# The first pair's neighbour codes are made and read earlier in a two-layer graph kernel

## What is computed

```
# layer 0: for every node the 25 neighbours of lowest number
h = max(layernorm(x), 0)
scores = where(adj != 0, -arange(N), -inf)
vals, idx = top_k(scores, 25)
feats = where(vals > -inf, h[idx], -inf)         # (b, n, 25, c)
agg = feats.max(axis=2)
agg = where(degree <= 25, max(agg, 0), agg)
x = x + relu(concat([h, agg]) @ W0 + b0)
# layer 1: dense masked attention over the same graph
h = max(layernorm(x), 0)
hidden = h @ W1.T;  a1, a2 = hidden @ a.T
attn = leaky_relu(a1[:, :, None] + a2[:, None, :], 0.2)
attn = softmax(where(adj > 0, attn, attn - 1e12))
x = x + attn @ hidden + bias1
```

## Time and profile before

| what | us |
|---|---|
| median of 3 runs | 5479.37 |
| the runs | 5475.32 to 5479.76 |
| the profiled execution's own time | 5479.48 |
| its span, first to last instruction | 5477.6 |
| busy: GpSimd | 3051.7 |
| busy: VectorE | 2618.6 |
| busy: TensorE | 2595.7 |
| busy: ScalarE | 1562.9 |

### The profile page before, as it was taken

The page is one execution under the profiler, slowest core; times in us unless marked ns, Lnnn a source line. Parts: engine busy times, 40 slices in busy tenths (PEclk is TensorE's granted clock), DMA queues, the critical chain, the costliest instruction groups (busy, mean ns, idle before and its releaser), DMA issues.

```text
span 5477.6 us, 38224 instructions
## 1 busy us (share of the span) xinstructions
PE 2595.7 (47%) x8782; PEld 1579.9 (29%) x8782; DVE 2618.6 (48%) x6725; ACT 1562.9 (29%) x1745; POOL 3051.7 (56%) x3204
## 2 busy tenths in 40 slices
PE   2212244455444455454455544455534555545479
PEld 1101122233222233332233322233322333323246
DVE  5444455454545454544454445444445445445342
ACT  3011133232333232333232333232323232323135
POOL 5566656555556555555555555655555656556520
PEclk9755566677767677766677766676766677767689
DMA  7344446555556565555565555555554655555320
GB/s 255 104 152 155 154 145 182 157 178 152 163 161 184 158 184 146 162 165 180 158 180 148 161 163 175 166 154 166 161 167 156 184 149 183 152 157 166 120 93 28
DMA packets 477228, 866.03 MB, mean 158 GB/s; under 512 B 308298, under 2 KB 309204, under 8 KB 456660
## 3 DMA queue, kind: packets, MB, share of 16 engines
q0 software_dynamic: 153600, 419.64, 27.0%
q1 hardware_dynamic: 305140, 378.64, 21.5%
q10 hardware_dynamic: 18432, 67.12, 3.1%
HBM read 690.98 MB, written 119.54 MB: 148 GB/s over the span
## 4 chain that ended last, share of the span: by engine, by line
another core or an unknown queue 31%; PE 21%; issue 16%; DVE 14%; ACT 13%; SPq 2%; DMA 1%; POOL 1%; ACTq 1%; DVEq 0%; POOLq 0%
PE acc L1325 11%; ACT nm_t L560 7%; DVE highest L909 3%; DVE top L843 2%; PE bank L1258 2%; DVE key L849 2%; ACT wgt L596 2%; SPq L364 2%; PE bank L1238 2%; PE pen L1318 1%; DVE stat L770 1%; PE pen L1317 1%; PE bank L1275 1%; POOL near L515 1%
## 5 line engine op out<-in xcount | busy, mean ns | idle before, releaser
L515 POOL DMA_INDIRECT near<-table_dram,idx x3200 | 3051.5, 954 | 2198.3 <-issue 996.5
L1325 PE MATMUL acc<-hid,wgt 128*128 (+1 forms) x4096 | 1094.5, 416 | 261.6 <-ACT wgt L596 225.9
L909 DVE TENSOR_TENSOR highest<-near,highest 128x512 f32<-128x512 f32 x1280 | 889.8, 695 | 149.6 <-DVE highest L909 65.1
L1325 PEld LDWEIGHTS acc<-hid,wgt 128*128 128x128 f32 x4096 | 836.0, 209 | 430.0 <-issue 208.5
L1258 PE MATMUL bank<-w_sb,h_t 128*128 128x256 f32 x1024 | 419.8, 581 | 692.2 <-ACT h_t L686 614.4
L925 DVE SCALAR_TENSOR_TENSOR x_q<-bank,x_q 128x256 f32<-128x256 f32 x128 | 54.2, 423 | 1081.7 <-PE bank L1260 854.2
L1258 PEld LDWEIGHTS bank<-w_sb,h_t 128*128 128x128 f32 x1024 | 286.4, 293 | 785.7 <-ACT h_t L686 639.5
L596 ACT ACTIVATE wgt<-pen,a_slope 128x512 f32<-128x512 f32 x448 | 304.2, 679 | 714.3 <-PE pen L1318 280.4
L560 ACT ACTIVATE nm_t<-adj_i,big_c 128x2048 bf16<-128x2048 int32 x128 | 499.2, 3951 | 5.0 <-DMA adj_i<-in_adj_dram 5.0
L843 DVE MAX8 top<-key 128x8 f32<-128x256 f32 (+1 forms) x1024 | 361.3, 387 | 255.6 <-remote 178.7
L686 ACT ACTIVATE h_t<-bank 128x512 f32<-128x512 f32 x128 | 75.9, 593 | 1401.8 <-remote 1020.9
(11 more groups left out here) (148 smaller groups left out, 2369.8 us busy)
## 6 DMA issues: line engine op xcount, KB each, us to landing
adj_i<-in_adj_dram SPq DMA_DIRECT2D x128, 1024.0 KB
nmask_dram<-nm_t ACTq DMA_DIRECT2D x128, 512.0 KB
nm_q<-nmask_dram SPq DMA_DIRECT2D x29, 2048.0 KB
near<-table_dram,idx POOLq DMA_INDIRECT x3200
h_q<-table_dram SPq DMA_DIRECT2D x32, 512.0 KB
x_q<-in_x_dram SPq DMA_DIRECT2D x32, 512.0 KB
xmid_dram<-x_q SPq DMA_DIRECT2D x32, 512.0 KB
o_q<-xmid_dram SPq DMA_DIRECT2D x32, 512.0 KB
```

The lines of the kernel that those rows point to most:

```text
L515: pool.indirect_dma_start(out=near[:, t % 2, k, :], out_offset=None, in_=table, in_offset=bass.IndirectOffsetOnAxis(ap=idx[:, t, k:k + 1], ...
L909: nc.vector.tensor_tensor(highest[:, :], pair(k), highest[:, :], ALU.max).then_inc(mx_step, 1)
L1325: mm = nc.tensor.matmul(acc[:, t, 0:C + 1], wgt_part(j)[:, t * P:(t + 1) * P], hid[:, bass.ds(batch * NJ + j, 1), 0:C + 1].rearrange("p a ...
```

## The change

Two calls move. On TensorE, `index_prep` of the first pair goes from behind attention's set-up to ahead of it. On VectorE, `index_words` of the first pair goes from behind the second tile's maximum to ahead of it; the rest of the pair's work stays behind that maximum. `selected` is called for the first pair only. Nothing is added or taken away.

```diff
--- before.py
+++ after.py
@@ -1148,7 +1148,6 @@
 
                 def selected(pair, between):
                     if "index" in stages:
-                        index_words(s + 1, pair)
                         index_rest(pair, between)
                     else:
                         between()
@@ -1161,6 +1160,8 @@
                 if "attend" in stages:
                     attend_setup(a, lo)
                 finished(0)
+                if "index" in stages:
+                    index_words(s + 1, 0)
                 gathered(1)
                 selected(0, third_tile)
                 finished(2)
@@ -1411,10 +1412,10 @@
                 if "project" in stages:
                     project(s - 1)
                 gathered(0)
+                if "index" in stages:
+                    index_prep(s + 1, 0)
                 if "attend" in stages:
                     attend_setup(a)
-                if "index" in stages:
-                    index_prep(s + 1, 0)
                 gathered(1)
                 for c in range(8):
                     if "attend" in stages:
```

## The result

The changed kernel takes 5275.57 us (median, 5258.32 to 5288.52), beside 5477.9 us for the kernel before (5475.32 to 5479.76): a ratio of 0.9635, 95% interval 0.9595 to 0.9674. The forecast was 5311 us. The profiled execution took 5279.74 us, 199.7 us less than that of before; its mean granted clock is 0.701 (before 0.708), so TensorE's clock has no part in the gain.

What follows compares the result with a forecast made beforehand. Bound: GpSimd's pauses waiting for other engines, chiefly 14.59 us at the fourth tile's ninth gather, 18 us of its chain being two late messages. 5479.5 - 192 + 24 = 5311 us; range 5222 to 5560, likeliest case 5250 to 5370.

Steps and rivals of the forecast that it cites:

- (1) to (3): TensorE's first-pair codes start 6.9 us earlier, taking 3.62; VectorE waits 3.7 us, then reads them in 1.5 to 2.2.
- (4): VectorE's second-tile maximum starts at 2540.6, lies wholly in the late stretch, takes 16.6 us and ends at 2557.2.
- (5): GpSimd, wanting the second tile's buffer at 2556.06, newly pauses there some 2 us.
- VectorE's `agg` 24 times: Sign of being right: GpSimd pauses of 1 to 4 us, ended by VectorE's `agg`, appear 24 times or more.
- (6): Attention's set-up moves back 5.9 us; penalties end near 2548, GpSimd asks near 2552, so 4 us of lateness are covered.
- (7): Second tile's transposes end at 2558.4, not 2561.2; the fourth tile's ninth gather comes earlier, gaining 8.0 us a step, 24 steps.
- Rival A: Message of the second tile's transposes stays late until GpSimd stops: 2.2 us a step lost, 5557 us; chance 0.25.
- (8): Steps where L861 does not wait are only delayed: 3 us in steps 1 to 3, 5 in 4, 27, 30; 24 together.
- rival D: All flows as in step 4 up to the ninth gather: 11.6 us gained a step, 5225 us; chance 0.12.

## Why the prediction was right, and where its steps were off

The forecast of 5311 us was 35 us above what came. The part of the mechanism that it named is borne out: of the two late messages between the second maximum and the ninth gather, the first left that path and the second is nearly prompt. Where GpSimd would stop instead it had wrong, and that the size came out so near is in part luck.

- (1) to (3) held: the codes' matmuls 3.60 us at their new place, L861 after 3.69 us of waiting, the three instructions 1.4 us (2.2 charged).
- (4) was mis-sized. It gave the second maximum 16.6 us, as if lateness began at a fixed point of the step. It lasts 13.4 us (1229.88 to 1243.29), less than the 14.5 of before: its gaps begin 3.6 us into it (1233.49), and 2.9 us into it before (medians of 22 steps; 2.9 to 6.0 and 2.2 to 3.8). The onset moved with the chain and is no fixed point of the step; what sets it is not shown.
- (5) failed as a place. No pause stands at the buffer's wait; "VectorE's `agg` 24 times" was wrong (5 times, and these are long pauses, 102.8 us in all). The new pause is at the penalties' wait, 4.1 us a step.
- (6) is the step that missed this. It counted the penalties' 6 us as covered by the 4 us left to GpSimd's question near 54 us into the step; they end at 53.2 and not near 50, since the row maxima's message is 4.7 us late, and their own message is late on top. The prediction let both pass as prompt.
- (7) was put at 8.0 us a step and measured 9.0. By place, the pause of 13.7 becomes 4.1 + 2.6, which is 7.0, and 2.2 come from the wait for the third tile's residual; the wait for the chunks moves from the 17th to the 23rd gather. Its reading (messages flow some 4 us after the gathers stop) fits ScalarE's copy, 3.95 us in 22 steps, but not L861 itself, whose message came 7.2 us ahead of the stop in the prediction's own rows, nor VectorE's rounds, held up until 6 us. GpSimd now stops 13 us earlier in the step, and the copy comes 3.8 us behind that stop; that the stop makes the gain is argued and not shown. Rival A needed the opposite, a message still late with the new stop added.
- (8): steps 1 to 3 grew from 155.3 to 157.4 us, 2.1 each, where 3 were charged; step 4 by 7.1 (137.2 to 144.3), where 5 were; steps 27 and 30 fell by 3.6 and 2.1, where 5 were charged to each. Together they cost 8 us, where 24 were charged.
- The sum: steps 5 to 26 gained 9.0 each, 197 us, and steps 28 and 29 gained 5.6 and 5.5, so 208 us where 192 were forecast; all the rest nearly cancels, and the execution became 199.7 us shorter. The two terms are off by 16 us each, in the same direction.

Two things the forecast did not have. It took late messages for a property of the kernel. They are not: on three chips they were absent and before took 4270 us, and on the one where the changed kernel ran unaltered it gained 0.13%. Nor is that rival D, "all flows", whose 5225 us still had the other pauses in it. And it argued from the stop that a message needs, but the only new stop that it gave the change was the 2 us of (5), shorter than the 4 us that it held necessary; its 8.0 us is a choice between two written-out steps, of which step 4 has stops shortly ahead of the ninth gather (2.44 and 3.15 us, rows 8) and step 27 has none.

What stays open is whether the stop or the new order brings the gain where messages are late: the runs with the stop alone and with the order alone all met prompt messages. For the stop speaks that the copy comes some 4 us behind it wherever it stands. For the order speaks that the codes are read at 40 us into the step, ahead of any stop, and that in step 27 of the kernel before, with the codes read at 47.5 us and no new stop, the pause is 5.28 us. Nor do the traces say what the messages queue behind.

## What to carry to other kernels

Where an engine's wait ends in a time that no instruction accounts for, look up what another engine stops doing just before it ends, and measure the distance in every step: here the gathers had stopped 3.95 us ahead of the copy, 22 times of 22. Then look for waits of the same kind that end without such a stop, before making a rule of it: here the codes' message came with the gathers running, also 22 times of 22. Work put ahead of such a late message can be nearly free (9.4 us for 2.1), so a late wait is not to be added up like work. And run the kernel before on more than one chip ahead of tuning such waits: a gain of 3.7% in one measurement (3.2% in another, with work added) was 0.1% where messages were prompt.

## What the runs showed of the hardware

- The same program took 5478 and 5486 us in two measurements (the first's chip is not on record, the second's is chip 4) and 4270, 4271 and 4269 us on three other chips (15, 2 and 10). GpSimd's time for a gather is 954 ns in the first and 958 on chip 2, and VectorE's and ScalarE's busy times agree within 1.2%; what differs is the waiting. TensorE's busy time is 2595.7 us against 2455.5, at a granted clock of 0.708 against 0.750; what of this is a consequence of the waiting was not tested.
- With late messages the second tile's maximum, 13 dependent VectorE operations, has gaps of some 0.7 us behind every one or two operations. They begin at the fourth to sixth operation before and the fifth to ninth in the changed kernel. The first tile's maximum has none (8.9 us), and neither has the chain of 13 built in as a delay (9.39 us).
- ScalarE's copy comes 3.8 to 4.0 us (medians) after GpSimd's last gather, behind runs of 26 gathers (the new stop) and of 37 (the ninth of the fourth tile) alike; VectorE's rounds are held up until 6.0 us after it, and L861's message arrives while gathers run. Where messages are prompt, 100 gathers a step without a pause make none late.
- The warning that the prediction took from the Trainium skill ("VectorE: DVE Perf Modes", The TRN2 errata), that dense semaphore increments of several engines should be spaced, is there a warning of a deadlock. None came in any run here. It speaks of no lateness, so rival A's 5557 us did not follow from it, and rival A did not come.
